# One decoder layer: the causal mask added in one matmul per bank, the experts' first weights split in every octet

## What is computed

```python
h = concat([pos_emb, nest_table[nesting], seg_table[segments]]) @ W
# attention on layernorm(h); with 128 tokens the mask is causal
q, k, v = x @ wq + bq, x @ wk + bk, x @ wv + bv
logits  = where(k_index <= q_index, (q / 8) @ k.T, -1e10)
h = h + softmax(logits) @ v @ wo + bo
# experts on layernorm(h)
logits = x @ router_w.T + router_b;  topk_val, topk_idx = top_k(logits, 2)
h1, h2 = split(x @ fc1_w[e].T + fc1_b[e], 2)          # 512 columns per expert
y      = (silu(h1) * h2) @ fc2_w[e].T + fc2_b[e]
out    = h + sum over the two chosen e of softmax(topk_val)[e] * y
```

## Time and profile before

| | |
|---|---|
| median of three runs | 1457.07 us |
| the profiled execution | 1445.55 us |
| its span, first to last instruction | 1443.5 us |
| TensorE busy | 1212.5 us, 84% of the span |
| VectorE busy | 1008.8 us, 70% |
| ScalarE busy | 985.7 us, 68% |
| GpSimd busy | 885.1 us, 61% |
| mean granted clock of TensorE | 0.968 |

### The profile page before, as it was taken

One profiled execution on the slowest core, in us unless ns is written; L12 is line 12 of the kernel. 1 busy time (PEld: TensorE's weight loads), 2 busy tenths in 40 slices (PEclk: granted clock), 3 DMA queues, 4 the chain that ended last, 5 costly groups with the idle time before them and its releaser, 6 DMA issues. The chain is left out here.

```text
span 1443.5 us, 47446 instructions
## 1 busy us (share of the span) xinstructions
PE 1212.5 (84%) x13916; PEld 1043.9 (72%) x13917; DVE 1008.8 (70%) x3837; ACT 985.7 (68%) x3496; POOL 885.1 (61%) x1214
## 2 busy tenths in 40 slices
PE   6898899999999899999999975678887777887885
PEld 4576777777777778777777764577777777777774
DVE  6578888888778788888878864656555555565553
ACT  3797898889879889888988863445444444454442
POOL 6346776667666667667667665555555545555554
PEclk9999999999999999999999996799999999999998
DMA  5240111111111111111111111434444334333431
GB/s 162 90 171 17 37 53 39 39 56 35 52 41 36 48 43 49 41 39 56 35 52 41 48 57 46 126 112 111 112 114 116 113 101 112 113 115 106 116 112 48
DMA packets 73348, 108.59 MB, mean 75 GB/s; under 512 B 15037, under 2 KB 39301, under 8 KB 73157
## 3 DMA queue, kind: packets, MB, share of 16 engines
q1 hardware_dynamic: 53444, 63.19, 15.8%
q0 software_dynamic: 19840, 44.62, 8.8%
HBM read 46.18 MB, written 53.18 MB: 69 GB/s over the span
## 5 line engine op out<-in xcount | busy, mean ns | idle before, releaser
L775 ACT ACTIVATE probs<-ps,neg_max 128x128 f32<-128x128 f32 (+1 forms) x1024 | 338.1, 361 | 20.1 <-DVE neg_max L963 17.7
L648 POOL DMA_INDIRECT xs<-normed,row x256 | 261.6, 1022 | 81.6 <-issue 78.7
L1247 PE MATMUL ps<-xT_hi,w_now 128*128 128x256 f32 x576 | 178.8, 310 | 93.4 <-DVE xT_lo L1134 92.6
L775 ACT ACTIVATION_READ_ACCUMULATOR probs<-ps,neg_max 128x1 f32 x1024 | 232.6, 227 | 0.0
L716 ACT CAST xT_hi<-ps 128x256 fp32r<-128x256 f32 x144 | 54.8, 381 | 247.6 <-PE ps L1410 225.7
L1247 PEld LDWEIGHTS ps<-xT_hi,w_now 128*128 128x128 f32 x576 | 109.6, 190 | 110.2 <-DVE xT_lo L1134 106.1
L587 POOL TENSOR_TENSOR probs<-probs,inv_sums 128x384 f32<-128x384 f32 x120 | 99.3, 828 | 124.1 <-DVE inv_sums L913 118.3
L1249 PE MATMUL ps<-xT_hi,w_now 128*128 128x256 f32 x576 | 162.8, 283 | 0.0
L1248 PE MATMUL ps<-xT_lo,w_now 128*128 128x256 f32 x576 | 162.7, 282 | 0.0
L684 POOL DMA_INDIRECT xs<-probs,v x108 | 104.4, 967 | 88.8 <-DVE probs L1143 62.1
L684 POOL DMA_INDIRECT out_h<-probs,v x108 | 104.5, 967 | 87.9 <-DVE probs L1143 60.8
(11 more groups left out here) (244 smaller groups left out, 3305.6 us busy)
## 6 DMA issues: line engine op xcount, KB each, us to landing
v<-xs SPq DMA_DIRECT2D x102, 260.0 KB
kT<-xs SPq DMA_DIRECT2D x34, 260.0 KB
xs<-pad_rows SPq DMA_DIRECT2D x16, 520.0 KB, 3.0
normed<-h SPq DMA_DIRECT2D x32, 256.0 KB
xs<-normed,row POOLq DMA_INDIRECT x256
w_parts<-in_w SPq DMA_DIRECT2D x1, 2048.0 KB, 9.0
xs<-probs,v POOLq DMA_INDIRECT x108
out_h<-probs,v POOLq DMA_INDIRECT x108
```

Of the source, the lines that this page charges most:

```text
L648: pool.indirect_dma_start((xs[0], xs_parts)[k], bass.IndirectOffsetOnAxis(ap=row[par][:, k, j:j + 1].bitcast(U32), axis=0), normed2[par][: ...
L775: ins = nc.scalar.activation(probs_p[par][:, half, slots[n]], ps[:, SCORES + half, slots[n]], ACT.Exp, bias=neg_max[par][:, half, n:n + 1] ...
L1247: T.matmul(dst, w_hi_, x_hi_, start=True, stop=False)
```

## The change

- **Mask.** The slots of a bank are reordered so that the masked keys of both halves of the queries are contiguous per half, 128 of them. Two matmuls per sequence, one per bank, replace the eight. Each has 64 rows, all 128 columns of the array and 256 moving columns. `ident_2` holds the 64 by 64 identity twice side by side; `causal` holds the triangle four times. The maximum and the reciprocals follow the new order with the same counts.
- **Weights.** `w1_parts` becomes two tensors, `w1_hi` and `w1_lo`, each contiguous. Every octet has one step w1_hi on ScalarE (in its second sequence) and one step w1_lo on GpSimd (in its sixth), each of 256 columns; in the last octet they stand in the first and second sequence. Two more semaphores are led, since the steps now run in the loop.
- **Second bias.** It is loaded as 8 partitions of 128 elements, split there on GpSimd, and two DMAs of SyncE write the two parts into rows 0 and 1 of `b2_parts`, whose clearing moves from the start to this step, with half of its columns. The matmul of L1428 reads the row twice by a broadcast.
- **Start.** The first eight small VectorE operations of the masks stand ahead of the wait for the tokens; the step xlo of the first group stands ahead of two additions of the second.

```diff
 octet_steps:
-            steps.append(("w1_hi", k))
-        if octets_done == 1:
-            steps.append(("w1_lo", k))
-            if k == 0:
-                steps.append(("b2_parts", k))
+        if octets_done == 1 and k == 0:
+            steps.append(("b2_parts", k))
+        if k == 1:
+            steps.append(("w1_hi", 0))
+        if k == 5:
+            steps.append(("w1_lo", 0))
 final_steps:
+        if k < 2:
+            steps.append((("w1_hi", "w1_lo")[k], 0))
 first_steps:
-    steps += [("norm", 0), ("normT", 0), ("embed", 1), ("embed_add", 1), ("embed_r", 1), ("xlo", 0), ("bias", 0)]
+    steps += [("norm", 0), ("normT", 0), ("embed", 1), ("xlo", 0), ("embed_add", 1), ("embed_r", 1), ("bias", 0)]
 tensors:
-        causal = sb("causal", [128, 3, HQ], BF16); ident_b = sb("ident_b", [128, 128], BF16)
+        causal = sb("causal", [128, 2, 2, HQ], BF16); ident_2 = sb("ident_2", [128, 2, HQ], BF16)
-        slots = (slice(0, S), slice(S, 2 * S), slice(2 * S, 2 * S + HQ), slice(2 * S + HQ, PACK))
+        slots = (slice(0, S), slice(S + HQ, 2 * S + HQ), slice(S, S + HQ), slice(2 * S + HQ, PACK))
-        w1_parts = sb("w1_parts", [D, EXPERTS, W1ROW], F32R)
+        w1_hi = sb("w1_hi", [D, EXPERTS * FC1], F32R); w1_lo = sb("w1_lo", [D, EXPERTS * FC1], F32R)
+        W1PART = EXPERTS * FC1 // octets
-        b2_parts = sb("b2_parts", [128, EXPERTS, 2, D], F32R)
-        part_rows = (slice(0, 1), slice(32, 33))
+        b2_raw = sb("b2_raw", [EXPERTS, D])
+        b2_split = sb("b2_split", [EXPERTS, 2, D], F32R)
+        b2_parts = sb("b2_parts", [128, EXPERTS, D], F32R)
 sync, in octet:
+                    if st[0] == "b2_parts":
+                        sp.wait_ge(s_b2, 1)
+                        for part in range(2):
+                            sp.dma_start(b2_parts[part:part + 1].bitcast(F32), b2_split[:, part].bitcast(F32)).then_inc(s_b2_in, 16)
 gpsimd, constants:
-            link(pool.tensor_copy(ident_b[:], ident[:]))
-            for n in range(3):
-                link(pool.tensor_copy(causal[:, n], triangle[:]))
+            for rows in (slice(0, HQ), slice(HQ, S)):
+                link(pool.tensor_copy(ident_2[rows], ident[rows, rows].unsqueeze(1).broadcast_to([HQ, 2, HQ])))
+            for n in range(4):
+                link(pool.tensor_copy(causal[:, n // 2, n % 2], triangle[:]))
-            link(pool.memset(b2_parts[:].bitcast(F32), 0.0))
 gpsimd, steps:
-                    pool.wait_ge(s_w1hi, i + 1)
-                    pool.tensor_tensor(w1_parts[:, i, FC1:W1ROW], w1_parts[:, i, FC1:W1ROW].bitcast(F32),
-                                       w1_parts[:, i, 0:FC1].bitcast(F32), ALU.subtract).then_inc(s_w1lo, 1)
+                    pool.wait_ge(w1hi_ready, LEAD + o + 1)
+                    carry_wait(pool)
+                    part = bass.ds(o * W1PART, W1PART)
+                    pool.tensor_tensor(w1_lo[:, part], w1_lo[:, part].bitcast(F32), w1_hi[:, part].bitcast(F32), ALU.subtract).then_inc(w1lo_ready, 1)
-                    for p in part_rows:
-                        ins = pool.tensor_copy(b2_parts[p], b2_raw[p].unsqueeze(2).broadcast_to([1, EXPERTS, 2, D]))
-                        link(ins)
+                    link(pool.memset(b2_parts[:].bitcast(F32), 0.0))
+                    link(pool.tensor_copy(b2_split[:, 0], b2_raw[:]))
+                    pool.tensor_tensor(b2_split[:, 1], b2_raw[:], b2_split[:, 0].bitcast(F32), ALU.subtract).then_inc(s_b2, 1)
 scalar, step w1_hi:
-                    nc.scalar.copy(w1_parts[:, i, 0:FC1], w1_parts[:, i, FC1:W1ROW].bitcast(F32)).then_inc(s_w1hi, 1)
+                    part = bass.ds(o * W1PART, W1PART)
+                    nc.scalar.copy(w1_hi[:, part], w1_lo[:, part].bitcast(F32)).then_inc(w1hi_ready, 1)
 tensor, step scores:
-                    for part in (slice(0, 3), slice(3, 4)):
-                        for c in range(2):
-                            for e in range(2):
-                                rows, wide = slice(e * HD, (e + 1) * HD), part.stop - part.start
-                                blocks = ps[c * HQ:(c + 1) * HQ, SCORES + e, 0:PACK].rearrange("p (n k) -> p n k", k=HQ)
-                                dst = blocks[:, 1:6:2] if wide == 3 else blocks[:, 4:5]
-                                ins = T.matmul(dst, ident_b[rows, rows], causal[rows, 0:wide], start=False, stop=True, skip_group_check=True)
+                    for e in range(2):
+                        rows = slice(e * HD, (e + 1) * HD)
+                        masked_keys = ps[:, SCORES + e, 0:PACK].rearrange("p (a k) -> p a k", a=2)[:, :, HQ:S + HQ]
+                        ins = T.matmul(masked_keys, ident_2[rows].rearrange("p c q -> p (c q)"), causal[rows].rearrange("p a n k -> p a (n k)"), start=False, stop=True,
+                                       skip_group_check=True)
```

More of the change, by code:

```diff
@@ L819, in _ @@
             act.wait_ge(s_b1, 16)
-            act.wait_ge(s_w1lo, EXPERTS)
+            act.wait_ge(w1lo_ready, LEAD + octets)
             act.wait_ge(numbers_ready, LEAD + 1)
@@ L853, in _, with place @@
             V = nc.vector
+            dve.wait_ge(s_const, 1)
+            p = small[:, 0:1]
+            acc, cmp_ = small[:, 1:2], small[:, 2:3]
+            n3 = PARTS * NEST
+            link(V.tensor_copy(part_code[:], p))
+            link(V.memset(acc, 0.0))
+            def place(edge, code_step, part_step):
+                link(V.tensor_scalar(cmp_, p, float(edge), None, ALU.is_ge))
+                link(V.scalar_tensor_tensor(part_code[:], cmp_, float(code_step), part_code[:], ALU.mult, ALU.add))
+                link(V.scalar_tensor_tensor(acc, cmp_, float(part_step), acc, ALU.mult, ALU.add))
+            edges = ((NEST, -NEST, 1), (2 * NEST, -NEST, 1), (n3, -NEST, -2), (n3 + SEG, -SEG, 1), (n3 + 2 * SEG, -SEG, 1))
+            for edge in edges[0:2]:
+                place(*edge)
             dve.wait_ge(s_x, 16)
@@ L873, in _ @@
             V.tensor_copy(codes_sb[:, 1], seg_int[:]).then_inc(s_codes, 1)
[L875 to L885 removed]
+            for edge in edges[2:]:
+                place(*edge)
             link(V.tensor_scalar(part_mask[:, PARTS:PARTS + 1], acc, 1.0, None, ALU.is_ge))
@@ L1195, in turn @@
                     dve.wait_ge(base_in[XBUFS - 1], LEAD + 16)
-            dve.wait_ge(s_w1hi, EXPERTS)
+            dve.wait_ge(w1hi_ready, LEAD + octets)
             dve.wait_ge(experts_ready, LEAD + 1)
@@ L1427, in fc2 @@
                 pe.wait_ge(y_ready, LEAD + n - 1)
-                T.matmul(ps[:, YB[z], 0:2 * D], add_parts[:], b2_parts[:, bass.ds(e, 1)].rearrange("p a r d -> p (a r d)"), start=True, stop=False,
+                T.matmul(ps[:, YB[z], 0:2 * D], add_parts[:], b2_parts[:, bass.ds(e, 1)].broadcast_to([128, 2, D]), start=True, stop=False,
                          skip_group_check=True)
@@ L1467, in _ @@
             turns = PH // XBUFS
[L1468 removed]
+            pe.wait_ge(s_b2_in, 16 * 2)
             pe.wait_ge(table_ready, LEAD + 1)
```

47 lines of the change are left out of this document (15 added, 32 removed).

## The result

The changed kernel takes 1446.57 us (median of six runs, 1441.68 to 1449.66), the kernel before 1456.93 (six runs, 1453.22 to 1458.69). The ratio is 0.9931, with an interval of 0.9908 to 0.9953: it is 10.4 us faster, where 5.4 us slower was forecast.

The account below looks back on a forecast made before the run. TensorE was taken to bound the attention octets, with no gap in ordinary sequences. Terms -1.6 - 8.5 - 1.5 + 2.5 + 14.5 = +5.4 us on the median 1457.07 gave 1462.5 us, range 1443 to 1472.

Parts of the forecast that it names:

- the spread: Weights' split steps in every octet: GpSimd's 256-column subtraction may hold VectorE up, 0.18 us per octet in 14 octets, +2.5 us.
- The forecast of the mask: Attention sequences on TensorE: one more change of array shape, 0.135 us per sequence, 17.3 us over 128, taken as +14.5 us.
- Rival D: Fourth change of shape paid but covered, ScalarE and VectorE setting the pace in more sequences; mask costs 6 us: 1454, chance 0.12.
- The fifth case: Inside all rivals: more idle time in the array may drop the granted clock in more octets, 3 us each; no own chance.
- start, first score matmul: Kernel start: GpSimd loses 2.04 + 0.25 us of memsets and gains 0.7, so -1.6 us (0 to 2.2).
- first octet: Eight ScalarE copies of 0.655 us removed; a little over a quarter of their 5.2 us gained, -1.5 us (0 to -4).
- second and third octet: GpSimd's eight subtractions and old bias split removed; octets fall from 58.6 to 51.1 and 52.0 to 51.0, -8.5 us.
- the fourth change of shape: TensorE, from 64 by 64 scores to the 64 by 128 mask: a fourth change per sequence, 0.135 us with its weight load.
- The bare weight load behind the change: TensorE, behind the mask's change of shape: first weight load not hidden, 0.04 us per sequence (bf16), where f32 took 0.05.
- rival B: Change of shape costs nothing, as only the rows' division counts; mask -2 us, sum -11 us: 1446, chance 0.20.
- L1358's 0.15 us: Sign in the profile: mask's first matmul about 0.15 us behind the last score matmul if right, 0.04 if the change is free.

Follow-up runs that it names:

- experiment 3: Old mask in the changed kernel: 0.9939 of before at level 1455; new mask in the kernel before: 0.9965. The long octet is from a profile of before.

## Why the prediction was wrong

**The step that failed** is the one on what bounds the kernel: "anything that TensorE gains or loses in a sequence is gained or lost in the whole". At the level at which the result was taken, the third sequence of most octets holds a wait for a late signal of TensorE, and its length jumps between classes by 0.9 to 1.7 us, the longest with a stretch at half clock. The mask and the spread together were to add 17 us, about 13 of them in the twelve loop octets. TensorE did pay its 0.10 us in the ordinary sequences, but the loop octets came out 0.3 us shorter each than the mean of four profiles of before (51.02 against 51.32), -3.6 us. By the profiles at this level the spread costs +7.6 us in the loop, the new mask gives -3.8 (against the changed kernel with the old one, one profile each), and before's octets at half clock, of which the changed kernel has none, are worth -7.3. The forecast of the mask, +14.5 us, is the term that turns the sign: without it the sum was -9.1, and -10.4 was measured. That these two lie so close is in part luck, since the spread was too cheap by 5 us and the half clock wasn't in the sum. The prediction had the earlier trace rows before it, took the 2.15 us for plain lateness of VectorE and said "perhaps". It also said that an ordinary sequence has no gap, where the earlier trace rows shows 0.20 us of idle time that ScalarE ended. Rival D named the cover (mask paid but covered, 0.12), with the wrong place and too small a size. The fifth case, more octets at half clock, came out the other way round.

**By terms**, at the level of 1263, where nothing jumps, the changed kernel against before with the new mask alone (both profiled there), and for the mask the timed pairs:

| term | forecast | measured |
|---|---|---|
| start, first score matmul | -1.6 | -1.1 |
| first octet | -1.5 | -0.6 |
| second and third octet | -8.5 | -9.8 |
| the spread in the loop | +2.5 | +8.2 |
| the mask | +14.5 | +3.9 to +7.6 |
| sum of the terms | +5.4 | +0.6 to +4.3 |
| the runs, by medians and by the ratio | | +3.6, +4.4 |

- *Second and third octet*: right, mechanism and size. 57.7 + 49.4 = 107.1 fell to 48.36 + 48.94 = 97.3. At 1455 they fell from 110.3 (mean of four) to 100.7, the one large gain that both levels share. Of the 9.8 us, 7.0 were the bias split's long copies on one partition, and 2.3 the weights' subtractions. The whole attention stage, first to last sequence, fell from 833.3 (mean of four) to 819.8 us; against the -10.4 us of the runs the difference is within the spread of the experts' stage.
- *Start*: right. Over six profiles with the old start the first score matmul stands at 38.9 us on average (38.2 to 40.0), over fourteen with the new one at 37.5 (36.7 to 38.0): -1.4.
- *First octet*: not resolved. With the eight copies it lasts 55.0 to 58.3 us, without them 55.1 to 58.5.
- *Spread*: right mechanism, size off by three. The forecast took 0.18 us per octet, a part of the 0.74, since it looked at L947 alone. The subtraction stood behind L615 and met a short copy in the chain to the scaling instead. Or, in every other octet or so, the instruction behind that. It stands still for all that is left of GpSimd's instruction, 0.4 to 0.6 us each time.
- *Mask*: right mechanism (the fourth change of shape, two matmuls side by side), 0.10 us and not 0.135, and in the whole not 85% of 128 such prices but 30% to 59% (3.9 and 7.6 of 12.8 us) at 1263. The bare weight load behind the change, counted at 0.04, did not show: the sequence grew by 0.10.

That the sum at the level of 1263 is near the forecast owes something to errors that cancel: the mask was too dear by 7 to 11 us, the spread too cheap by 6.

**The range** (1443 to 1472) held the time, but only because it reached to rival B. B's own reason, a free change of shape, is refuted by L1358's 0.15 us.

**Still open**: what makes TensorE's signals late at one level and not at the other. The traces with late signals also hold a third fewer semaphore records (about 14,000 against 21,000), so that the records and the lateness may have one cause; no run here tells. Open too is why the half clock nearly vanishes with the change, and whether the experts' stage is a few us longer with the weights in two tiles at the level of 1455: at 1263 it is not (385.4 to 387.5 us in all kernels), at 1455 its spread of 16 us hides it, and within a set before lies among the others (524.6 us beside 521.3 to 525.9).

## What to carry to other kernels

A wait that the profile puts down to an engine is to be followed one step further: if that engine was itself idle, waiting for the first one's signal, the time is neither engine's work, and a cost beside it may vanish or jump. A small GpSimd instruction beside VectorE can cost VectorE nearly its own length (0.4 to 0.6 of 0.74 us here), and the chain behind it as much, so it is to be placed where VectorE is idle, or given to VectorE. And one profiled execution against one is no account of a stage: the experts' stage alone differed by 16 us between executions, more than the whole effect.

## What the runs showed of the hardware

- One kernel ran at 1263 and at 1452 us on the same chip in different sets of runs, with instructions of equal length. The late signals of TensorE are the one difference found: 0.31 us behind the start of the matmul against about 1.0 in the experts' stage, where the two engines wait for it in each block. The casts of the experts' input in one stretch of 80 us, changed kernel, level 1455 and then 1263 (idle time and what ended it behind the bar):

```profile
L719 ACT CAST xT_hi<-ps 128x256 fp32r<-128x256 f32 x22 | 8.4, 382 | 40.3 <-PE ps L1421 36.9 <-remote 3.4
```

```profile
L719 ACT CAST xT_hi<-ps 128x256 fp32r<-128x256 f32 x30 | 11.2, 374 | 13.5 <-PE ps L1421 13.0
```

- A change of the array's shape that keeps the rows and changes the columns, from 64 by 64 to 64 by 128, costs 0.11 us beyond the streaming, like the others (0.09 to 0.11 in the earlier trace rows); two more of them with 0.05 us of streaming (128 columns) cost 0.30 us per sequence.
- In the long octet of experiment 3 the granted clock falls from 2.4 to 1.2 GHz for 3.4 us at 273.2, right behind TensorE's wait of 2.18 us; the octet takes 53.9 us in place of 50.7. But nine other waits of 2.15 to 2.24 us in the profiles of before passed at full clock, and their octets took 50.4 to 50.9 us.
- Where a GpSimd instruction runs, a short VectorE instruction can stand still until it ends: 0.76 us in place of 0.16 and 0.61 in place of 0.18 beside a subtraction of 0.74 to 0.78 us.
